# Half of two layer-norm applications moved from VectorE to GpSimd, an input buffer released earlier, and statistics moved to other PSUM banks

## What is computed

```python
q = x @ Wq.T; v = x @ Wv.T                 # 16 heads of 128
ret = scan(v)                              # state = lam * state + v_t, per head
out = layernorm(q * ret) * silu(x @ Wg.T)
x = layernorm(x + out @ Wo.T)              # the "second norm" below
w = normalised top-2 of sigmoid(x @ Wgf.T) # 8 experts, dense over tokens
ffn = sum_e w_e * (silu(x @ W1_e.T) * (x @ W3_e.T)) @ W2_e.T
x = layernorm(x + ffn)                     # the "third norm" below
```

## Time and profile before

| what | value |
|---|---|
| median of 3 runs | 4662.12 us (4658.76 to 4664.65) |
| the profiled execution's own time | 4662.31 us |
| its span on the slowest core, the one shown | 4659.7 us |
| spans of the eight cores | 4649.2 to 4659.7 us |
| PE busy | 3958.1 us, 85% of the span |
| VectorE (DVE) busy | 1207.7 us, 26% |
| ScalarE (ACT) busy | 351.2 us, 8% |
| GpSimd (POOL) busy | 318.7 us, 7% |
| mean granted TensorE clock | 0.917 |

### The profile page before, as it was taken

One profiled execution on the slowest core, in us unless ns is written; L12 is line 12 of the kernel. 1 busy time (PEld: TensorE's weight loads), 2 busy tenths in 40 slices (PEclk: granted clock), 3 DMA queues, 4 the chain that ended last, 5 costly groups with the idle time before them and its releaser, 6 DMA issues.

```text
span 4659.7 us, 46492 instructions; the slowest of 8 cores (4649.2 to 4659.7 us)
## 1 busy us (share of the span) xinstructions
PE 3958.1 (85%) x17449; PEld 1698.0 (36%) x17449; DVE 1207.7 (26%) x2019; ACT 351.2 (8%) x622; POOL 318.7 (7%) x602
## 2 busy tenths in 40 slices
PE   5698847379999999999959984736999999999994
PEld 1243313134444444444414331312444444444441
DVE  0122061621211211211262206153121121121126
ACT  0002101000000000000010210100000000000001
POOL 2100000000000000000010000000000000000000
PEclk8699969689999999999979996967999999999997
DMA  9843325424754444444464331642465444444442
GB/s 160 135 77 53 62 41 140 122 50 73 126 91 69 76 73 73 77 73 69 72 136 77 59 59 39 137 118 52 72 119 96 69 77 73 73 77 73 69 77 76
DMA packets 132168, 388.97 MB, mean 83 GB/s; under 512 B 15216, under 2 KB 15216, under 8 KB 131952
## 3 DMA queue, kind: packets, MB, share of 16 engines
q0 software_dynamic: 85392, 302.06, 39.5%
q1 hardware_dynamic: 37344, 67.17, 5.1%
q10 hardware_dynamic: 9216, 16.78, 1.0%
HBM read 654.42 MB, written 33.55 MB: 148 GB/s over the span
## 4 chain that ended last, share of the span: by engine, by line
PE 79%; DVE 9%; DMA 5%; issue 4%; ACT 2%; DVEq 0%; POOL 0%; SPq 0%; ACTq 0%; POOLq 0%
PE ps L948 20%; PE ps L1019 19%; PE ps L966 19%; PE ps L631 5%; PE ps L492 5%; PE ps L563 5%; PE ps L703 4%; DMA wring<-xpre 2%; DVE ntmpS L664 1%; DVE ygS L672 1%; DVE x1tS L716 1%; DVE ot2S L1107 1%; DVE ntmpS L658 1%; PE ps L925 1%; DMA xf32S<-x1hbm 1%
## 5 line engine op out<-in xcount | busy, mean ns | idle before, releaser
L948 PE MATMUL ps<-xnS,wring 128*128 128x512 bf16 x4096 | 935.7, 388 | 0.0
L966 PE MATMUL ps<-xnS,wring 128*128 128x512 bf16 x4096 | 904.9, 379 | 0.0
L1019 PE MATMUL ps<-gbufS,wring 128*128 128x512 bf16 x4096 | 886.4, 379 | 0.0
L948 PEld LDWEIGHTS ps<-xnS,wring 128*128 128x128 bf16 x4096 | 407.1, 100 | 522.5 <-issue 60.8
L1019 PEld LDWEIGHTS ps<-gbufS,wring 128*128 128x128 bf16 x4096 | 400.2, 98 | 484.9 <-issue 3.5
L966 PEld LDWEIGHTS ps<-xnS,wring 128*128 128x128 bf16 x4096 | 400.6, 98 | 483.5
L988 DVE TENSOR_TENSOR gtmpS<-ps,sh1S 128x512 bf16<-128x512 f32 x256 | 176.1, 688 | 1466.5 <-PE ps L966 1466.5
L703 PE MATMUL ps<-ygS,wring 128*128 128x512 bf16 x1024 | 258.9, 410 | 122.5 <-DVE ygS L672 122.5
L981 ACT ACTIVATE sh1S<-ps 128x512 bf16<-128x512 f32 x256 | 138.9, 594 | 2361.9 <-PE ps L948 2361.8
L631 PE MATMUL ps<-xnS,wring 128*128 128x512 bf16 x1024 | 239.1, 388 | 48.1 <-ACT ygS L644 30.9
L492 PE MATMUL ps<-xnS,wring 128*128 128x512 bf16 x1024 | 232.3, 386 | 48.9 <-ACT vS L519 35.4
(11 more groups left out here) (126 smaller groups left out, 1460.6 us busy)
## 6 DMA issues: line engine op xcount, KB each, us to landing
wring<-w1T POOLq DMA_DIRECT2D x128, 512.0 KB, 5.1
wring<-w3T POOLq DMA_DIRECT2D x128, 512.0 KB, 5.1
wring<-w2T POOLq DMA_DIRECT2D x128, 512.0 KB, 5.1
xf32S<-x1hbm SPq DMA_DIRECT2D x128, 256.0 KB, 4.6
wring<-xpre POOLq DMA_DIRECT2D x48, 512.0 KB, 9.8
xf32S<-xfm SPq DMA_DIRECT2D x64, 256.0 KB, 6.6
wring<-wvT POOLq DMA_DIRECT2D x32, 512.0 KB, 6.1
wring<-wqT POOLq DMA_DIRECT2D x32, 512.0 KB, 6.1
```

Source lines behind the costliest of these rows:

```text
L948: g1 = pr.step("pe", lambda en, kt=kt, c=c, slot=slot1: en.matmul(out=psS[c][:, 0:CW], lhsT=wringS[slot][:, kt * P:(kt + 1) * P], rhs=x1nS ...
L966: g3 = pr.step("pe", lambda en, kt=kt, c=c, slot=slot3: en.matmul(out=psS[2 + c][:, 0:CW], lhsT=wringS[slot][:, kt * P:(kt + 1) * P], rhs= ...
L1019: grp = pr.step("pe", lambda en, k=k, c=c, slot=slot2: en.matmul(out=psS[4 + c][:, 0:CW], lhsT=wringS[slot][:, k * P:(k + 1) * P], rhs=gbu ...
```

## The change

The second norm and the third norm are applied by VectorE for the even feature tiles and by GpSimd for the odd ones; in the second norm the multiply becomes a plain tensor_tensor. The guard of `xnS` (`xn_b`) is released by the last W3 matmul of the half's feed-forward instead of the last W2 matmul. The broadcasts of the second norm go through PSUM banks 6 and 7 instead of 0 and 1, and the statistics of the third norm into banks 4 to 7 instead of 0 to 3.

```diff
-            bt2 = bcast_rows(t_mu2, t_rs2, 0, 1)
+            bt2 = bcast_rows(t_mu2, t_rs2, 6, 7)
...
             for kt in range(KT):
+                eng = "dve" if kt % 2 == 0 else "pool"
...
-                    tn1 = pr.tick("dve", lambda en, xslot=xslot, c=c, ntslot=ntslot: en.tensor_tensor(
+                    tn1 = pr.tick(eng, lambda en, xslot=xslot, c=c, ntslot=ntslot: en.tensor_tensor(
...
-                    tn2 = pr.tick("dve", lambda en, kt=kt, c=c, ntslot=ntslot: en.scalar_tensor_tensor(
+                    tn2 = pr.tick(eng, lambda en, kt=kt, c=c, ntslot=ntslot: en.tensor_tensor(
                         out=xnS[:, kt * TH + c * CW:kt * TH + (c + 1) * CW],
                         in0=ntmpS[:, ntslot * CW:(ntslot + 1) * CW],
-                        scalar=1.0,
                         in1=rstdB[:, c * CW:(c + 1) * CW],
-                        op0=ALU.mult, op1=ALU.mult),
+                        op=ALU.mult),
...
                         wb3.read(g3)
+                        ffn_last_g3 = g3
...
-                xn_b.read(grp_last)
+
+            xn_b.read(ffn_last_g3)
...
-                        dep0 += psB[0 + c].begin_write()
+                        dep0 += psB[4 + c].begin_write()
...
-                        dep1 += psB[2 + c].begin_write()
+                        dep1 += psB[6 + c].begin_write()
...
-            t_mu3, t_rs3 = ln_rows(st3_sum + st3_sq, 0, 2)
+            t_mu3, t_rs3 = ln_rows(st3_sum + st3_sq, 4, 6)
...
             for ht in range(KT):
+                eng3 = "dve" if ht % 2 == 0 else "pool"
...
-                    tn1 = pr.tick("dve", lambda en, ht=ht, c=c, otslot=otslot: en.tensor_tensor(
+                    tn1 = pr.tick(eng3, lambda en, ht=ht, c=c, otslot=otslot: en.tensor_tensor(
...
-                    tn2 = pr.tick("dve", lambda en, otslot=otslot, c=c: en.tensor_tensor(
+                    tn2 = pr.tick(eng3, lambda en, otslot=otslot, c=c: en.tensor_tensor(
```

More of the change, by code:

```diff
@@ L1079, in emit_half @@
                     if ht == 0:
-                        dep0 += psB[0 + c].begin_write()
+                        dep0 += psB[4 + c].begin_write()
                     st3_sum[c] = pr.step("pe", lambda en, ht=ht, c=c, cbslot=cbslot: en.matmul(
-                        out=psS[0 + c][0:1, 0:CW], lhsT=onescol_bf[:],
+                        out=psS[4 + c][0:1, 0:CW], lhsT=onescol_bf[:],
                         rhs=gtmpS[:, cbslot * CW:(cbslot + 1) * CW],
@@ L1088, in emit_half @@
                     if ht == 0:
-                        dep1 += psB[2 + c].begin_write()
+                        dep1 += psB[6 + c].begin_write()
                     st3_sq[c] = pr.step("pe", lambda en, ht=ht, c=c, sqslot=sqslot: en.matmul(
-                        out=psS[2 + c][0:1, 0:CW], lhsT=onescol_bf[:],
+                        out=psS[6 + c][0:1, 0:CW], lhsT=onescol_bf[:],
                         rhs=sh1S[:, sqslot * CW:(sqslot + 1) * CW],
@@ L1096, in emit_half @@
             for c in range(NCW):
-                psB[0 + c].wrote(st3_sum[c])
-                psB[2 + c].wrote(st3_sq[c])
-            t_mu3, t_rs3 = ln_rows(st3_sum + st3_sq, 0, 2)
+                psB[4 + c].wrote(st3_sum[c])
+                psB[6 + c].wrote(st3_sq[c])
+            t_mu3, t_rs3 = ln_rows(st3_sum + st3_sq, 4, 6)
             bt3 = bcast_rows(t_mu3, t_rs3, 4, 5)
             for ht in range(KT):
+                eng3 = "dve" if ht % 2 == 0 else "pool"
                 for c in range(NCW):
```

## The result

The changed kernel is slower: its time is 1.0188 of the kernel before, with an interval of 1.0167 to 1.0209, or +87.6 us on 4660. The prediction said 4755 us, +93, with a range of 4690 to 4800; the ratio gives 4747.6. In some executions of either kernel one die ran at a lower clock and took longer; they are left out of every comparison here. Its span is 4745.7 us against 4659.7 before, 86.0 more.

What follows compares the result with a forecast made beforehand. TensorE holds 79% of the chain, so stretches where it waits for VectorE's norms count. The terms 14.4 + 8.9 + 56.7 + 13.0 gave +93.0 us on the profiled 4662.3: 4755 us, range 4690 to 4800.

Steps and rivals of the forecast that it cites:

- the term S: Duration of GpSimd's share of each split norm: 57.9 us, the middle between 49.6 (no exclusion) and 66.2 (full exclusion).
- four stretches of the sum: Second norm half 0 +14.4, second norm half 1 +8.9, border of the halves +56.7, end of the kernel +13.0 us.
- the exclusion: In the norms, whether VectorE's and GpSimd's instructions block each other in SBUF; undecided by the rows, so the middle was taken.
- the rings: Buffer slots around the norms: GpSimd's first tile waits 1.4 us for a ntmpS slot, once in each second norm.
- The input loads behind GpSimd's share: At the border, half 1's 16 loads queue behind GpSimd's norm work and lose their cover: 57 us, the largest term.
- the 2.35 us that the prediction gave back: At the border, the second V group runs warm, 6.91 us instead of 9.26, so 2.35 us are saved.
- the rival with S = 66.2: Full exclusion in the norms: the two engines' instructions alternate, 0.69 + 1.38 us a pair; +126, 4788 us; chance 0.15.
- the estimate of 1.12 us: GpSimd's two-input norm instruction priced from the skill page: a share of 41.4 us, +27 us in total; not used.
- The second norms and the end: Three split norms outside the border: +14.4 us in half 0, +8.9 in half 1, +13.0 at the end.
- The 50.4 us from which the forecast subtracted: Length of half 1's second norm before the change, some of it waits for loads; its term was S + 1.4 - 50.4.
- Banks and release at nothing: The moved PSUM banks and the earlier release of the input buffer were each forecast to cost or gain 0.
- 4S - 138.6: The prediction's total change in us over all four stretches; +93.0 for S = 57.9.

Runs made afterwards that it cites:

- e9: Kernel before, all norms on VectorE, but half 1's input loads wait for the last multiply of half 0's third norm: span 4700.9 us, 41.2 over the kernel before.
- e2: Changed kernel with only half 0's third norm back on VectorE alone: 4687.4 us median, 1.0032 of the kernel before.
- e11: Changed kernel with half 1's 16 input loads and first four weight groups issued before half 0's third norm: 1.0069 of the kernel before.
- e4: Changed kernel, VectorE reading the norms' broadcasts from PSUM, half 0's third norm on VectorE alone: 4657.4 us median, 0.9981 of the kernel before.
- e5: Kernel before with the early release of the input buffer alone: span 4660.5 us against 4659.7, no ratio.
- e6: Kernel before with the moved PSUM bank numbers alone: 0.9972 of the kernel before (0.9928 to 1.0016).

## Why the mechanism was right and the size of one term was not, step by step

*The step that failed.* It is the term S, GpSimd's share of a norm, which stands in all four stretches of the sum. It was put at 57.9 us, and it measured 54.7 in both third norms, counted from VectorE's first subtract (GpSimd itself starts 1.5 us before it), and 54.9 and 53.9 in the second norms (less the 1.4 of the first slot). Three things in it were wrong, and they partly cancel: GpSimd's instruction (1.38 us put, 1.26 measured alone), the exclusion (put as half of the collisions at 2.07 us a pair, when most instructions collide, at 1.67 a pair), and the rings (put at one wait of 1.4 us, when both engines wait again and again). That the total came within 7 us of the forecast is in part luck. Where each comes from is said below.

*The input loads behind GpSimd's share.* Right in mechanism, and the largest term. The place of the loads was forecast at 2443 and is 2452.23, the landing to which TensorE waits at 2480 and is 2487.98; the norm began 12.2 us later in this trace (2397.52 against 2385.30), so relative to it both are a little earlier than forecast. From the start of the norm to the second V group, the forecast was S + 52.4 = 110.3 us and it took 107.2: GpSimd's share is 3.2 shorter (54.7 for 57.9), load and landing 1.3 shorter (35.75 for 37.1), and the first V and Q groups 1.5 longer (16.8 for 15.3). The chain of the changed kernel ends this at the next V group:
```profile
2487.98 9.87 PE ps L492 x32
...
2504.76 6.91 PE ps L492 x32
```
The second takes 6.91 us, where in the earlier trace rows it took 9.26: the 2.35 us that the prediction gave back. The first takes 9.87, where 8.35 had been assumed. It came after 91 us of idle, and the windows of this core show the granted clock behind PE, PEld, DVE, ACT and POOL busy: 0.50, which is 1.2 GHz, in the idle time, and 0.68 on average over the group.
```profile
2455.00:2485.00 30.00, 0.00 (x0) 0.00 (x0) 0.00 (x0) 0.00 (x0) 7.85 (x15) 0.50 1.04 157
2488.00:2497.00 9.00, 9.00 (x29) 3.46 (x30) 0.00 (x0) 0.00 (x0) 0.00 (x0) 0.68 0.64 119
```
That is where the 1.5 us are. Three runs bear the term out from different sides: e9 makes it alone, e2 takes GpSimd's work away, and e11 takes only the order away.

*GpSimd's price and the exclusion.* GpSimd's operation is 1.26 us, not 1.38. The exclusion is real, as the rival with S = 66.2 had it, but a pair costs less than the sum. Where nothing else waits, starts of VectorE's instructions are 1.67 us apart in the third norm, where 0.69 + 1.26 is 1.95. In half 0, 28 of VectorE's 32 instructions in the third norm and 21 of 32 in the second take longer than alone. So the forecast's middle was near, but not because half the instructions collide: most do, and a collision costs less than was feared. The prediction had no row to decide this; e4 decided it. A part of each instruction that touches no SBUF tile could explain the missing 0.28 us. No run tried that, so it stays open.

*The rings.* They were put at 1.4 us once in each second norm and at nothing in the third. In the second norm of half 0 VectorE waits seven times for GpSimd to free a slot of ntmpS, 8.6 us in all. In the third norms GpSimd waits for stores to free ot2S, 5.2 us in half 0 (the longest 3.5) and 5.4 in half 1, and VectorE 3.0 and 4.3. GpSimd's 32 instructions hold 48.8 us of half 0's third norm and 46.2 of its second; the rest of the share is waiting and the short gap between instructions. No run took the rings away from the even split, so what they alone added to S is open.

The Trainium skill (SBUF, State Buffer, section Who interferes with whom) says that a VectorE instruction with two SBUF inputs and a GpSimd instruction that reads SBUF block each other. The trace agrees on who meets whom: 1.56 to 1.74 us with two such inputs, 0.687 with one (e4). It does not fit a block for the whole of each instruction: by that a pair would take 1.95 us, and it took 1.67. The rival built on it deserved more than 0.15, at 1.67 a pair and not at the 2.07 that it was priced with.

The Trainium skill (GPSIMD Engine Reference, section 3.1) has 4497 ns for 2048 columns, a quarter of which was the estimate of 1.12 us for GpSimd's operation; measured is 1.26. The estimate is 11% low; half of the tensor_scalar row, which the sum used, was 9.5% high (1.38).

*The second norms and the end.* Half 0's second norm and the end were over-forecast by 3.2 and 2.4 us, which is S: 11.2 for 14.4, 10.6 for 13.0. In half 1 the sum of norm and FFN is right (+9.2 for +8.9), but only 4.6 of it stand between the first subtract and the router; the other 4.6 are in the FFN behind (1474.9 before, 1479.5 now). In e9, whose norms are those of the kernel before, the norm took 47.05 and the FFN behind 1479.05, 1526.1 together, and the kernel before had 52.3 + 1474.9 = 1527.2. So these two trade time, and only their sum is to be read. The 50.4 us from which the forecast subtracted hold about 5 us of waits that e5, e6 and e9 do not have in their norm of 47.1; yet norm and FFN together take hardly less there, 1526.1 to 1526.6. With the norm of those runs the term would have been 14.1, so that +8.9 met +9.2 is luck too.

*Banks and release at nothing.* Right for both as far as e6 and e5 can tell. The release is not idle in itself: in e5 it lets the loads go 26 us earlier, in e2 27 us against the norm. They were hidden already, so it buys nothing.

*The sum.* 93.0 forecast, 86.0 measured by span and 87.6 by ratio. With S = 55 the prediction's own 4S - 138.6 gives 81.4: 11.5, 6.0, 53.8 and 10.1 for the four stretches, against 11.2, 9.2, 53.9 and 10.6. The one large remainder, 3.2 us in half 1's second norm, comes from its base of 50.4: with the 5.2 us shorter norm of e5, e6 and e9 the term is 11.2, and 2.0 too high instead, which I can't name. Another 1.0 lies outside the change, where cores differ by as much.

## What to carry to other kernels

Before moving work to an idle engine, list what its instruction queue holds behind that work: here DMA issues that had been free stood 54.7 us behind arithmetic, and cost more than the arithmetic did in all three other places together. Two engines do not halve a stage unless the split goes by their prices (here 0.69 to 1.26, so two tiles to one) and unless their instructions can run at the same time; a second operand in PSUM was enough for that. After a stage has become faster, look for what it now waits for: here the ring of output slots took back 12 us until the result was written in place.

## What the hardware showed that was not expected

VectorE and GpSimd, alternating on 128x512 fp32 tiles with two SBUF inputs each, took 1.67 us a pair, 0.28 less than the sum of their times alone (0.69 and 1.26). A GpSimd subtract of that shape, with two inputs, costs 1.26 us, 2.5 ns a column, and its one-input tensor_scalar (8 partitions, 1024 columns) cost 2.7. Letting 16 loads start 26 us sooner (e5) changed neither the border nor, by much, the waits for stores beside it (3.8 us, 4.4 before); with every load and matmul out of the norm (e9) these waits are gone.
